# Graph adjacency from one-hots on a Trainium2 core: GpSimd weights a pair of edge columns in one operation, or in two

## What is computed

```python
deg = segment_sum(ew, col_f, N)                      # weighted in-degree, self loops with weight 1
norm = dinv[row_f] * ew * dinv[col_f]
out = segment_sum((xn @ W)[row_f] * norm[:, None], col_f, N) + b
q, k, v = split(xn @ w_qkv, 3);  q = elu(q) + 1;  k = elu(k) + 1
kv = einsum('bhnd,bhnm->bhdm', k, v)                 # and its normaliser, then @ w_out + b_out
```

## Time and profile before

| | |
|---|---|
| median of 3 executions | 677.27 us (676.73 to 680.25) |
| the profiled execution | 679.04 us, span from first to last instruction 677.3 us |
| TensorE busy (matmul) | 589.4 us, 87% of the span |
| VectorE busy | 488.2 us, 72% |
| ScalarE busy | 314.1 us, 46% |
| GpSimd busy | 253.9 us, 37% |
| mean granted TensorE clock | 0.939 of full |

### The profile page before, as it was taken

The page is one execution under the profiler, slowest core; times in us unless marked ns, Lnnn a source line. Parts: engine busy times, 40 slices in busy tenths (PEclk is TensorE's granted clock), DMA queues, the critical chain, the costliest instruction groups (busy, mean ns, idle before and its releaser), DMA issues.

```text
span 677.3 us, 8694 instructions
## 1 busy us (share of the span) xinstructions
PE 589.4 (87%) x2964; PEld 471.1 (70%) x2964; DVE 488.2 (72%) x1001; ACT 314.1 (46%) x598; POOL 253.9 (37%) x239
## 2 busy tenths in 40 slices
PE   1698998989999979999739996599989997999687
PEld 1486886767778658888626776488867876666486
DVE  6758988979996977866578984466576555676655
ACT  4467866867756421121115552243545773311370
POOL 5556766756785234545485002100010220010060
PEclk9899989999999989999957996599998998999989
DMA  9200000000010200030121000000020000200004
GB/s 323 91 1 0 2 1 1 1 0 1 1 63 1 62 16 31 32 76 25 63 91 41 2 1 0 0 1 0 0 79 1 0 1 1 78 1 0 1 0 152
DMA packets 15043, 21.09 MB, mean 31 GB/s; under 512 B 3260, under 2 KB 6000, under 8 KB 15002
## 3 DMA queue, kind: packets, MB, share of 16 engines
q1 hardware_dynamic: 13674, 17.94, 8.1%
q10 hardware_dynamic: 1328, 2.62, 1.1%
HBM read 18.00 MB, written 2.56 MB: 30 GB/s over the span
## 4 chain that ended last, share of the span: by engine, by line
PE 69%; DVE 19%; issue 4%; ACT 4%; POOL 1%; DVEq 1%; DMA 1%; ACTq 0%; POOLq 0%
PE p L1761 9%; PE pQ L1868 4%; PE p L1611 4%; PE p L1868 4%; PE pH L1627 3%; PE pQ L1627 3%; PE p L1627 3%; PE p L1843 2%; DVE onehot L1123 2%; PE pH L2011 2%; PE p L1949 2%; PE pQ L2011 2%; PE pKV L1656 2%; PE pH L1773 2%; PE pQ L1773 2%
## 5 line engine op out<-in xcount | busy, mean ns | idle before, releaser
L867 POOL TENSOR_TENSOR Loh<-onehot,whl 128x512 fp32r<-128x512 f32 x85 | 89.6, 1054 | 46.1 <-DVE onehot L1123 46.1
L1123 DVE TENSOR_SCALAR onehot<-iota_src,srclo 128x128 fp32r<-128x128 f32 x170 | 75.0, 481 | 0.7 <-DVE flagint L1135 0.7
L1761 PE MATMUL p<-G,ATs 128*128 128x512 f32 x300 | 71.2, 396 | 1.2 <-DVE G L1263 1.2
L1611 PEld LDWEIGHTS p<-Roh,Loh 128*128 128x128 f32 x340 | 48.4, 192 | 30.8 <-issue 26.7
L1761 PEld LDWEIGHTS p<-G,ATs 128*128 128x128 f32 x300 | 57.4, 192 | 14.0 <-issue 2.0
L1611 PE MATMUL p<-Roh,Loh 128*128 128x200 f32 x340 | 53.5, 280 | 11.7 <-POOL Loh L867 4.9
L984 POOL TENSOR_TENSOR xT<-xn,xT 128x512 fp32r<-128x512 f32 x10 | 13.0, 1302 | 118.9 <-ACT xT L709 118.8
L517 ACT ACTIVATE away<-iota_key,key 128x200 f32<-128x200 f32 x85 | 38.7, 456 | 24.8 <-PE p L1611 24.8
L1627 PE MATMUL pQ<-wsl,xT 128*128 128x512 f32 x168 | 47.3, 410 | 1.4 <-DVE xT L1039 1.4
L1627 PE MATMUL pH<-wsl,xT 128*128 128x512 f32 x168 | 46.5, 405 | 0.0
L885 POOL TENSOR_TENSOR ATs<-AT,ATs 128x1280 fp32r<-128x1280 f32 x10 | 29.6, 2961 | 37.8 <-ACT ATs L573 37.7
(11 more groups left out here) (547 smaller groups left out, 1459.1 us busy)
## 6 DMA issues: line engine op xcount, KB each, us to landing
xb<-in_x SPq DMA_DIRECT2D x9, 256.0 KB, 2.7
out<-nodes SPq DMA_DIRECT2D x9, 256.0 KB
wraw<-in_L_mix_w_qkv ACTq DMA_DIRECT2D x2, 1024.0 KB, 7.7
qbuf<-in_L_mix_w_qkv SPq DMA_DIRECT2D x2, 1024.0 KB, 6.3
nodes<-in_x SPq DMA_DIRECT2D x1, 1024.0 KB, 9.1
wraw<-in_L_mix_w_qkv SPq DMA_DIRECT2D x1, 1024.0 KB, 11.3
wraw<-in_L_gnn_W SPq DMA_DIRECT2D x1, 1024.0 KB, 13.5
raw<-in_L_mix_w_out SPq DMA_DIRECT2D x1, 1024.0 KB, 5.3
```

What stands on the lines that cost most here:

```text
L867: pool.tensor_tensor(Loh[:, g % SLOTS], o, w, ALU.mult).then_inc(S["oh_pool"], 1)
L1123: ins = v.tensor_scalar(onehot_[:, g % SLOTS, c, :], iota_src[:], srclo[:, 2 * g + c:2 * g + c + 1], None, ALU.is_equal)
L1611: ins = pe.matmul(pW[g % 2][:, 0:T * WIN], Loh[:, g % SLOTS, c, part, :], Roh[:, g % RSLOTS, c, :], start=(c + part == 0), stop=(c + part ...
L1761: ins = pe.matmul(pG[u][:, :], ATs[:, u, x, s_, :], G[:, y, s_, :], start=(s_ + n == 0), stop=(s_ == T - 1 and n == 2))
```

## The change

GpSimd's multiplication is cut in two, one operation of 256 values for each column. The first waits for the one-hot of column 0 alone: VectorE now counts `oh_src` up after each column. TensorE's wait for `oh_pool` moves into the loop over columns: column 0's two products wait for the first operation, column 1's two for the second. The counts of all later users of the two semaphores are doubled.

```diff
@@ semaphore counts
-                ("cmb_ok", "ksb_ok", 1), ("z_one", "oh_src", CP), ...
+                ("cmb_ok", "ksb_ok", 1), ("z_one", "oh_src", 2 * CP), ...
@@ sync
-            sp.wait_ge(S["oh_pool"], CP)
+            sp.wait_ge(S["oh_pool"], 2 * CP)
@@ gpsimd
             for g in range(CP):
-                pool.wait_ge(S["oh_src"], g + 1)
-                w = whl[:, 2 * g:2 * g + 2, :].bitcast(F32).rearrange("p c (k n) -> p c k n", n=1).broadcast_to([P, 2, 2, P])
-                o = onehot_[:, g % SLOTS].bitcast(F32).rearrange("p c (k n) -> p c k n", k=1).broadcast_to([P, 2, 2, P])
-                pool.tensor_tensor(Loh[:, g % SLOTS], o, w, ALU.mult).then_inc(S["oh_pool"], 1)
+                for c in range(2):
+                    pool.wait_ge(S["oh_src"], 2 * g + c + 1)
+                    w = whl[:, 2 * g + c, :].bitcast(F32).rearrange("p (k n) -> p k n", n=1).broadcast_to([P, 2, P])
+                    o = onehot_[:, g % SLOTS, c].bitcast(F32).rearrange("p (k n) -> p k n", k=1).broadcast_to([P, 2, P])
+                    pool.tensor_tensor(Loh[:, g % SLOTS, c], o, w, ALU.mult).then_inc(S["oh_pool"], 1)
@@ vector, onehots(g)
                 for c in range(2):
-                    ins = v.tensor_scalar(onehot_[:, g % SLOTS, c, :], iota_src[:], srclo[:, 2 * g + c:2 * g + c + 1], None, ALU.is_equal)
-                ins.then_inc(S["oh_src"], 1)
+                    v.tensor_scalar(onehot_[:, g % SLOTS, c, :], iota_src[:], srclo[:, 2 * g + c:2 * g + c + 1], None, ALU.is_equal).then_inc(S["oh_src"], 1)
@@ tensor, adj(g)
-                pe.wait_ge(S["oh_pool"], g + 1)
                 if g >= 2:
                     pe.wait_ge(S["a_acc"], g - 1)
                 for c in range(2):
+                    pe.wait_ge(S["oh_pool"], 2 * g + c + 1)
                     for part in range(2):
```

More of the change, by code:

```diff
@@ L301, in build @@
                 ("nu_hi", "h_out", T), ("q1_hi", "w_hi", 3), ("u1_hi", "wo_hi", 0), ("zt_hi", "kvt_hi", 1),
-                ("cmb_ok", "ksb_ok", 1), ("z_one", "oh_src", CP), ("mw_hi", "m_hi", 4), ("kt_hi", "g_hi", T), ("a2_hi", "ats_hi", T),
+                ("cmb_ok", "ksb_ok", 1), ("z_one", "oh_src", 2 * CP), ("mw_hi", "m_hi", 4), ("kt_hi", "g_hi", T), ("a2_hi", "ats_hi", T),
                 ("r2_hi", "qt_hi", T), ("g2_hi", "fw_hi", FFL), ("vt_hi", "ft_ok", 3), ("n_ps", "xt_ps", T),
```

## The result

The changed kernel took **682.57 us**, the median of 20 runs (678.71 to 687.24); the kernel before, run beside it on the same chip, 677.49 (20 runs, 672.43 to 683.02). The ratio is 1.0078, with a 95% interval of 1.0056 to 1.0100: slower by 0.8%, or 5.1 us. Ratios leave out executions over 1.5% above the fastest of the same kernel, medians are over all. The time is inside the predicted range and above the 679.3 forecast; it is the time of rival A, 682.0. The forecast growth was 2.0 us, so the range held only because it reached as far as rival A.

A forecast was written before the change was run, and what follows sets the result against it. The prediction took the stage to be limited in turn by TensorE and by VectorE with GpSimd behind it. Delays of +5.5 less gains of 1.8 and 1.7 gave +2.0 us on the median 677.27: 679.3, range 674.0 to 683.0.

The forecast's parts named there:

- rival A: Slower: the delay before q_elu isn't absorbed and VectorE starts the next run late; 21 places, +4.7 us, 682.0; chance 0.27.
- What bounds the kernel: The stage is limited in turn by TensorE, busy 129.33 of 141 us, and by VectorE with GpSimd behind it.
- Half an operation: GpSimd's multiplication of 256 values takes 0.61 us, bounds 0.53 and 0.74; two in a row overlap by 0.04.
- The start: GpSimd's first half starts 0.08 us after the first one-hot's end, at 0.36; the second ends at 1.54, against 1.60 before.
- Roh: VectorE's Roh of column 1 is held until GpSimd's first half ends; VectorE's next instruction is 0.38 to 0.39 us late.
- rival B: Roh starts ahead of GpSimd's first half, which waits up to 0.19 us; VectorE loses nothing: -2.3 us, 675.0; chance 0.18.
- The chain: In chains of waiting pairs, a pair takes 1.34 us in place of 1.41; counted at 26 pairs, 1.8 us gained.
- TensorE's early start: Column 0's products go ahead once their half is there: 0.33 us gained in 5 of 7 runs of waiting pairs, 1.7 us.
- The count of places: Where k_elu, v_lo or q_elu follows on VectorE, 0.39 us is added: 14 of 21 places counted, 5.5 us.
- Rival C: A GpSimd half has no fixed cost and takes 0.53 us, so chains shorten to 1.18: 674.0; chance 0.12.
- The waits that I costed at nothing: TensorE's 85 added waits for GpSimd's halves cost nothing where the half is there; upper bound 6.8 us in all.

The follow-up runs named there:

- complement kernel: The change, with Roh ahead of the source one-hots at all pairs but the 20 that k_elu, v_lo or q_elu follows: 681.33 us, 1.0041.
- late-started kernel: The change, but both GpSimd halves wait for both source one-hots: 677.58 us, 0.9973 to the kernel before; in a repeat 680.01 us, 1.0038.

## Why the prediction was right or wrong

**What bounds the kernel** was read rightly, as two limits in turn, TensorE and VectorE. That balance was what the change used up: the earlier trace rows showed VectorE only 14 us from full.

**Half an operation:** 0.61 taken, 0.62 measured, and 0.04 of overlap. Right. The Trainium skill's page "GPSIMD Engine Reference" has the 2.5 cycles a value in its section "Instruction dispatch"; the section that the prediction names has about 2.6. Estimates by either, 0.72 and 0.74 for a half, lie above the measured 0.62.

**The start:** 0.08 after the first one-hot's end. Right: 134.20 against Roh's 134.24.

**Roh:** held until the first half's end, 0.38 to 0.39 late. Measured 691 - 314 = 0.377 in the mean. Right, and rival B with it excluded: 84 of 85 Rohs took 0.7 us, and the one that didn't is the first, at 53.22, which began 0.04 ahead of GpSimd's operation. The Trainium skill's page "SBUF — State Buffer", section "Who interferes with whom", says that the one who issues first keeps the port pair for its whole instruction; the trace agrees here down to 0.04 us.

**The chain:** 1.34 a pair predicted, 1.37 measured. The mechanism was right, and small: 0.04 on 26 pairs is 1.0 us, not 1.8. Even that didn't show: in the kernel with Roh first at the places alone, where chains run at the new pace and nothing is lost, the stage is 139.7, as before. Whether the gain is there and something else takes it was not isolated.

**TensorE's early start:** 1.7 us of gain predicted. This step failed, and the rows ahead of the prediction could have told it. It rested on 5 runs of waiting pairs that begin with a wait for Loh. But the pair at 158.08 waited for an addition as well: that ended at 157.45 + 0.35 = 157.80, only 0.03 before Loh's 157.83. The five runs stand like this in the trace of the kernel before: their first pairs, at 107.61, 130.20, 153.76, 174.38 and 194.13, start 0.28 after an addition and 0.25 after Loh, and they hold 3.2 of the 4.9 us of waits for Loh. So an earlier Loh could gain 0.03 there, not 0.33: then the addition, which the halves don't bring forward, ends last. In the changed kernel 0.2 us of waits for Loh are left of 4.9, and TensorE waits as long or longer, for the additions. The kernel that waits for the whole pair again had a stage 0.7 shorter, not 1.7 longer.

**The count of places** is the step that decided: 14 x 0.39 = 5.5 us, with q_elu's third absorbed by the idle 0.81 of the earlier trace rows. It can be counted in the trace of the changed kernel: behind 15 of the 20 places a pair of TensorE waits and starts 0.25 us after the end of the first addition that follows. They are 5 of the 7 k_elu, all 7 v_lo and 3 of the 6 q_elu. (The other two of the 17 long waits, at 116.46 and 146.44, were there before the change, at 115.55 and 144.76.) If each passes its delay on in full, that is 15 x 0.38 = 5.7 us, an estimate, beside 5.9 measured. So the count of 14 was near, though partly by luck: two k_elu cost nothing, and three q_elu were not absorbed. One of these is the very place of the stretch that the prediction showed, since the pair at 158.08 waits for the addition behind q_elu and not only for its one-hots; in the changed kernel it is the pair at 160.54, 0.25 after the addition's end at 160.29. By the complement kernel 4.6 of the 5.9 us belong to the 20 places, and what shares the remaining 1.3 was not isolated. What was wrong was to take 3.5 us of gains off the 5.5. With 5.5 and no gains the forecast would have been 677.27 + 5.5 = 682.8.

**Rival A** gave 682.0 by a sum of other parts (21 places, the same gains): the right mechanism of VectorE starting each run late, but the right time by luck, since too many places and gains that didn't come cancelled. It deserved more than 0.27, since VectorE's 90% was noted for it. **Rival C** fell with the half's 0.62.

**The waits that I costed at nothing** cost nothing: the kernel without them is as slow.

## What to carry to other kernels

Before an operation that shares GpSimd's and VectorE's access is started earlier, look which VectorE instruction will stand first behind its start: the price is that instruction's delay, and it is paid only where nothing was held before. Before a gain is taken from a wait, look when the instruction's other operands were ready: if one came 0.03 us earlier, 0.03 us is the gain. The releaser that a profile names is the last of several, and may hide such a neighbour. Where two engines share the pace of a stage, compare stage lengths at like granted clock, since the medians of one and the same kernel lay 0.4 to 0.7% apart here from one set of executions to the next (677.58 and 680.01, 676.2 and 680.83), nearly what the change did.

## What the runs showed of the hardware that was not expected

- **0.04 us decide, and always the same way.** GpSimd's start at 134.20 held the Roh of 134.24, and 84 of 85 Rohs were held, the longest 703 ns; in the late-started kernel the median was 311. Which instruction is held follows from the order of VectorE's three: with the whole Loh and Roh first, Roh took 1.045 us in the median.
- **TensorE starts later after the same addition** when another semaphore stands behind the accumulator's: 0.25 us (135.81 to 136.06) against 0.14 before. It is the time that followed Loh before. With the order put back the waiting pairs start 0.15 after the addition, in all four kernels that have it, and in three comparisons that was worth 0.5 or 0.6 us of a stage.
- **Two GpSimd operations for one** took 1.20 us in place of 1.05, and with the loss of Roh away that cost nothing measurable.

What stays open: where the shorter chains' gain goes, whether the shorter times of two kernels in their first runs (0.9973 and 0.9957) were more than spread, and the 1.3 us between the 20 places' share and the whole. No version was shown to beat the kernel before.
